# A gated cross-attention kernel on one Trainium2 core: two of its layer norms are computed inside the attention stages

## The reference

```python
def _layernorm(x, axis=-1, eps=1e-05):
    m = jnp.mean(x, axis=axis, keepdims=True)
    v = jnp.var(x, axis=axis, keepdims=True)
    return (x - m) / jnp.sqrt(v + eps)

x = x + jnp.tanh(g_xattn[0]) * _L0_xattn_ref(_layernorm(x), ctx_4096, Wq, Wk, Wv, Wo)
x = x + jnp.tanh(g_ffn[0]) * _L0_ffn_ref(_layernorm(x), W, b, Wq, Wk, A, Bm)
x = x + jnp.tanh(g_xattn[1]) * _L1_xattn_ref(_layernorm(x), ctx_4096, mask, Wq, Wk, Wv, Wo, q_norm_w, k_norm_w)
x = x + jnp.tanh(g_ffn[1]) * _L1_ffn_ref(_layernorm(x), ...)
```

```python
result = jnp.einsum('bsi,oi->bso', x, W) + b
q, k = x @ Wq.T, x @ Wk.T                    # (B, S, 8, 32) each
w = softmax(sum(q * k, -1) / sqrt(32), -1)
h = jnp.einsum('bsi,eri->bser', x, A)
return result + jnp.einsum('bse,bser,eor->bso', w, h, Bm)
```

## Time and profile before

| | us |
|---|---|
| median of 3 runs | 2628.84 (2624.82 to 2633.49) |
| profiled execution, whole | 2625.69 |
| its span, first to last instruction | 2623.9 |
| mean granted TensorE clock | 0.952 of 2.4 GHz |
| busy: PE, DVE, ACT, POOL | 2405.3, 1481.2, 1075.4, 995.0 |

### The profile page before, as it was taken

One profiled execution on the slowest core, in us unless ns is written; L12 is line 12 of the kernel. 1 busy time (PEld: TensorE's weight loads), 2 busy tenths in 40 slices (PEclk: granted clock), 3 DMA queues, 4 the chain that ended last, 5 costly groups with the idle time before them and its releaser, 6 DMA issues. The chain is left out here.

```text
span 2623.9 us, 34763 instructions
## 1 busy us (share of the span) xinstructions
PE 2405.3 (92%) x13032; PEld 2210.6 (84%) x13032; DVE 1481.2 (56%) x2352; ACT 1075.4 (41%) x2444; POOL 995.0 (38%) x812
## 2 busy tenths in 40 slices
PE   8999999979998899999879689999999999999724
PEld 6888888768998789998769578999999999999713
DVE  6222222132300566776677557777777777777797
ACT  3221222122311466667431245555555555554413
POOL 3000000000000446565253167667677677665110
PEclk9999999989999899999989899999999999999757
DMA  6222222143323223222213123333333333322001
GB/s 204 68 66 69 73 69 69 49 168 105 113 83 90 69 71 92 88 90 69 88 60 104 56 72 93 104 101 99 106 99 97 109 98 99 109 85 82 6 0 50
DMA packets 161240, 224.35 MB, mean 86 GB/s; under 512 B 31718, under 2 KB 124290, under 8 KB 160050
## 3 DMA queue, kind: packets, MB, share of 16 engines
q1 hardware_dynamic: 161074, 222.14, 27.2%
HBM read 183.81 MB, written 38.29 MB: 85 GB/s over the span
## 5 line engine op out<-in xcount | busy, mean ns | idle before, releaser
L967 POOL TENSOR_TENSOR attend_w_hi<-attend_w_raw,attend_one 128x1024 fp32r<-128x1024 f32 (+1 forms) x178 | 333.3, 1872 | 155.9 <-DMA attend_w_raw<-in_wo 81.5
L1146 DVE TENSOR_TENSOR attend_w_lo<-attend_w_raw,attend_w_hi 128x1024 fp32r<-128x1024 f32 (+1 forms) x184 | 252.4, 1372 | 206.3 <-ACT attend_w_hi L1034 123.1
L1284 PE MATMUL attend_ps_gemm<-normed_hi,attend_w_hi 128*128 128x400 f32 x704 | 246.5, 350 | 28.9 <-DVE attend_w_lo L1146 28.9
L1050 ACT ACTIVATE attend_p<-attend_p,attend_neg_max 100x361 f32<-100x361 f32 x256 | 150.9, 591 | 258.2 <-DVE attend_neg_max L1185 258.2
L1284 PE MATMUL attend_ps_gemm<-attend_o_hi,attend_w_hi 128*128 128x400 f32 x704 | 250.1, 355 | 4.4 <-issue 4.4
L1284 PE MATMUL attend_ps_gemm<-normed_lo,attend_w_hi 128*128 128x400 f32 x704 | 244.3, 347 | 0.0
L1284 PE MATMUL attend_ps_gemm<-normed_hi,attend_w_lo 128*128 128x400 f32 x704 | 243.5, 346 | 0.0
L1284 PE MATMUL attend_ps_gemm<-attend_o_hi,attend_w_lo 128*128 128x400 f32 x704 | 243.2, 346 | 0.0
L1284 PE MATMUL attend_ps_gemm<-attend_o_lo,attend_w_hi 128*128 128x400 f32 x704 | 243.2, 345 | 0.0
L301 DVE TENSOR_TENSOR context_k_square<-context_k_rows 128x512 f32<-128x512 f32 (+1 forms) x46 | 31.8, 691 | 346.7 <-ACT context_k_rows L226 346.6
L1059 ACT ACTIVATE attend_p<-attend_p,attend_exp_inv 100x361 f32<-100x361 f32 (+1 forms) x384 | 207.7, 620 | 0.0
(11 more groups left out here) (281 smaller groups left out, 6384.9 us busy)
## 6 DMA issues: line engine op xcount, KB each, us to landing
attend_w_raw<-in_wq SPq DMA_DIRECT2D x88, 512.0 KB, 4.0
attend_w_raw<-in_wo SPq DMA_DIRECT2D x64, 512.0 KB, 4.1
middle_w_raw<-in_wf SPq DMA_DIRECT2D x26, 512.0 KB, 3.5
attend_w_raw<-in_wo SPq DMA_DIRECT2D x32, 384.0 KB, 3.6
context_ctx_raw<-in_ctxT SPq DMA_DIRECT2D x8, 1456.0 KB, 7.2
attend_k_raw<-scratch_k SPq DMA_DIRECT2D x64, 180.5 KB, 3.6
context_ctx_raw<-in_ctxF SPq DMA_DIRECT2D x22, 512.0 KB
scratch_v<-context_v_out SPq DMA_DIRECT2D x44, 256.0 KB, 2.2
```

Of the source, the lines that this page charges most:

```text
L967: pool.tensor_tensor(hi, w_flat(w_raw, j % RAW, j), one[:hi.shape[0]].to_broadcast(hi.shape), ALU.mult).then_inc(w_hi_done, 1)
L1050: act.activation(p[:, slot, h], p[:, slot, h], ACT.Exp, bias=neg_max[:, slot, h:h + 1], accum_out=exp_sum[:, slot, h:h + 1]).then_inc(expe ...
L1146: dve.tensor_tensor(w_flat(w_lo, j % SPLIT, j), w_flat(w_raw, j % RAW, j), w_flat(w_hi, j % SPLIT, j).bitcast(F32), ALU.subtract).then_inc ...
L1284: mm = pe.matmul(out, left[a](c), right[b](c), start=(c == 0 and a == b == 0), stop=(c == chunks - 1 and a == 1))
```

## The change

The norms move by one half of the tokens. In layer 0's attention the units 18 to 31 compute the norm of the **first** half for the feed-forward, on POOL (sums, centring, scaling, remainders) and ACT (squares, root, rounding), with the reciprocal on DVE and two matmuls on PE. In `middle` remain two norms of four: that of the second half of its own input (made beside the first half's products) and that of the first half of layer 1's input (made beside the second half's products). In layer 1's attention the units 1 to 20 compute the norm of the **second** half of its own input, here with centring, scaling and remainders on DVE; the queries of that half start at unit 25 and wait for it. The mean and variance matmuls get places of their own in the ring of the two PSUM banks. Within `middle` the turn of the softmax weights moves from behind tile 5 to behind tile 6, `extra` starts behind tile 7, and DVE's list is reordered. POOL no longer waits for a norm ahead of its first weights.

```diff
+    if layer == 0:
+        NORM_HALF, C_SLOTS = 0, 4
+        ADD_AT, MEAN_AT, CENTRE_AT = (18, 19, 20, 20), 20, (21, 21, 22, 22)
+        SQUARE_AT, GATHER_AT, FOLD_AT = (22, 23, 24, 25), (24, 25, 26), 26
+        VAR_AT, INVERT_AT, SCALE_AT, HIGH_AT, LOW_AT = 26, 27, (27, 28, 28, 29), (28, 29, 29, 30), (30, 30, 31, 31)
+    else:
+        NORM_HALF, C_SLOTS = 1, 3
+        ADD_AT, MEAN_AT, CENTRE_AT = (1, 2, 3, 4), 5, (6, 7, 8, 9)
+        SQUARE_AT, GATHER_AT, FOLD_AT = (7, 8, 9, 10), (9, 10, 11), 12
+        VAR_AT, INVERT_AT, SCALE_AT, HIGH_AT, LOW_AT = 13, 14, (15, 16, 17, 18), (16, 17, 18, 19), (17, 18, 19, 20)
...
@@ attend, gpsimd @@
+            def add_tokens(k):
+                if layer == 0 and k < PAIRS - 1:
+                    pool.wait_ge(o_read, NU - 2 * HB + 4 + 2 * k)
...
+            def centre(k):
+                pool.wait_ge(mean_copied, 1)
+                pool.tensor_tensor(centred[:, k], norm_pair(tokens, k), norm_stat[:, 0].unsqueeze(1).to_broadcast([P, 2, HT]),
+                                   ALU.subtract).then_inc(centred_done, 1)
+
+            def scale(k):
+                pool.wait_ge(norm_inverted, 1)
+                pool.tensor_tensor(centred[:, k], centred[:, k], norm_stat[:, 1].unsqueeze(1).to_broadcast([P, 2, HT]), ALU.mult
+                                   ).then_inc(norm_scaled, 1)
...
                 for j in output_tiles(u + 1)[1:] + query_tiles(u + 1):
                     weights(j)
+                for k in range(PAIRS):
+                    if u == ADD_AT[k]:
+                        add_tokens(k)
+                    if k and u == GATHER_AT[k - 1]:
+                        add_squares(k)
+                if u == FOLD_AT:
+                    fold_squares()
+                if layer == 0:
+                    for k in range(PAIRS):
+                        if u == CENTRE_AT[k]:
+                            centre(k)
+                        if u == SCALE_AT[k]:
+                            scale(k)
+                        if u == LOW_AT[k]:
+                            remainder_normed(k)
                 squares(query_of(u))
@@ attend, scalar, at the end of a unit @@
+                for m in range(PAIRS):
+                    if u == SQUARE_AT[m]:
+                        square_centred(m)
+                    if u == HIGH_AT[m]:
+                        round_normed(m)
                 copy_q(query_of(u))
+                if u == MEAN_AT:
+                    copy_mean()
+                if u == VAR_AT:
+                    root_variance()
@@ attend, vector, at the end of a unit @@
+                if u == INVERT_AT:
+                    invert_root()
+                if layer == 1:
+                    for m in range(PAIRS):
+                        if u == CENTRE_AT[m]:
+                            centre(m)
+                        if u == LOW_AT[m]:
+                            remainder_normed(m)
+                        if u == SCALE_AT[m]:
+                            scale(m)
                 remainder_q(query_of(u))
@@ attend, tensor @@
+                if layer == 1 and n == G * QT:
+                    pe.wait_ge(ln_lo_done, PAIRS)
...
+            def norm_gemm(kind):
+                at = gemm_at[kind, 0, 0]
+                pe.wait_ge(norm_added, PAIRS if kind == "mean" else 2 * PAIRS)
+                bank_free(at)
+                pe.matmul(ps_gemm[:, at % 2, :HT], mean_w[:], norm_sum[:, 0], start=True, stop=True).then_inc(gemm_done, 1)
...
                 queries(query_of(u))
+                if u == MEAN_AT:
+                    norm_gemm("mean")
+                if u == VAR_AT:
+                    norm_gemm("var")
@@ middle, gpsimd @@
-            pool.wait_ge(ln_lo_done, PAIRS)
             for j in range(EARLY, EARLY + 3):
                 weights(j)
@@ middle, tensor @@
             pe.wait_ge(consts, CONSTS)
-            for c in range(NC):
-                mean_part(0, c)
-            mean(1)
-            variance_parts(0)
             for s in range(2):
                 for t in range(TILES):
                     product(s, t)
                     if s == 1 and t == 0:
                         extra(0, NC - 1)
-                    if s == 1 and t == 2:
-                        mean(2)
-                    if t == (3 if s == 0 else 7):
-                        variance(s + 1)
+                    if t == 1 + s:
+                        mean(s)
                     if t == QK:
                         score(s)
-                    if t == QK + 1:
+                    if t == QK + 2:
                         turn(s)
-                    if t > QK + 1:
+                    if t == QK + 3:
+                        extra(s, 0)
+                        extra(s, 1)
+                    if t > QK + 3:
                         extra(s, t - QK - 2)
-                    if s == 1 and t >= QK + 4:
-                        pe.wait_ge(o_read, NC + t - QK - 3)
-                        mean_part(3, t - QK - 4)
+                    if t == QK + 4:
+                        variance(s)
             extra(1, NC - 1)
-            for c in range(TILES - QK - 4, NC):
-                pe.wait_ge(o_read, NC + c + 1)
-                mean_part(3, c)
-            variance_parts(3)
```

317 lines of the change are left out of this document (188 added, 129 removed).

## The result

The changed kernel takes 2597.19 us (median of 4 runs, 2596.77 to 2599.51), the kernel before 2628.38 in the same comparison: 31.2 us less, ratio 0.9882 with a 95% interval of 0.9864 to 0.9899 (27 to 36 us). The forecast was 2590, 37 us less: the right size, 7 us too good, and just outside the interval.

The account below looks back on a forecast made before the run. PE bounds the attention stages, while serial chains starve it in three places of `middle`. Terms -45.9 + 6.5 + 2.4 = -37.0 us give 2588.7 from the profiled execution, 2591.8 from the median; forecast 2590, range 2577 to 2606 us.

Parts of the forecast that it names:

- Part 1: Start of `middle`: without norm 0, the first weight tile's remainder sets the products' start at 1307.8, 20.2 us earlier.
- the list of signs: What the changed profile should show, such as `middle`'s first product 7 to 8 us after the block's start.
- Part 2: Products of `middle`: 142.95 us become 137.7, with the `spread` wait gone and 6.4 us of new waits.
- Part 3: End of `middle`: next block begins at 1448.0 instead of 1493.95; 45.9 us saved in `middle`.
- Part 4: Layer 0's units 18 to 31: the added norm work is mostly covered and costs 6.5 us.
- my fourth rival: Layer 0's end: last two remainders behind POOL's last weights move the block's end up to 4 us; 2594 us; 0.62 with forecast.
- Part 5: Layer 1's units 1 to 20: the norm costs 2.4 us, 1.2 of it matmuls.
- The first: Rival: `middle` goes better and the cover in layer 0 holds; about 2581 us; chance 0.15.
- The second: Rival, both attention stages: each added POOL operation blocks a remainder 1.9 us, PE sees half; about 2611 us; chance 0.18.
- third: Rival: POOL becomes the bound of the attention units, so the kernel is slower; about 2642 us; chance 0.03.
- The -37.0: Whole kernel: sum of the stage terms, -45.9 + 6.5 + 2.4 us.

Follow-up runs that it names:

- no_norm3: Kernel before without norm 3, the norm behind the first feed-forward's last output tile for the next block's first half: 2606.73 us.
- Experiment 6: Changed kernel with POOL's last two norm remainders in layer 0's unit 31 moved ahead of the last output tiles' weights: 2596.48 us.
- experiment 12: Doses: changed kernel with one to four extra 128x800 additions on POOL or DVE in layer 1 units without norm work: 2603.86 us.
- the four moves: Changed kernel with unit 27's reciprocal and POOL's last layer 0 remainders earlier, `middle`'s squares sum behind tile 8's remainder, second-half mean one tile later: 2584.61 us.
- experiment 2: Changed kernel without the norm work in layer 0's units 18 to 31: 2588.03 us.
- experiment 3: Changed kernel without the norm work in layer 1's units 1 to 20: 2594.63 us.
- experiment 5: Changed kernel with DVE's reciprocal in layer 0's unit 27 moved ahead of its wait for o_hi: 2594.95 us.

## Why the prediction was nearly right

**Part 1, the start of `middle`: right.** By the sum the first product was to come 6.8 us behind the block's start, and it stands 6.3 behind it (the list of signs said 7 to 8, which didn't follow from the sum). That the first weights would be what is late next could be read from the rows of before.

**Part 2, the products: the term that was mis-sized.** I had 137.7 us, the profiled execution has 143.0 from first product to last add. The sum of the waits was right, 6.2 against 6.4 us, their places only in part: before tile 8 there are 2.43 and 1.21 (forecast 2.7 each), and 2.57 stand before the mean of the second half, which I had not as a wait at all. In the earlier trace rows the chain ran beside POOL; its shapes take 3.4 us alone and up to 8.3 beside three of POOL's roundings, so the one place came out shorter than I took it and the other appeared. What I left out wholly is the clock behind the waits. I allowed 1.6 us for it behind the wait that went, and nothing behind those that came. Two falls are 3.0 us of the 5.3 in this execution, the cold start another 0.9 (7.5 us for the first tile instead of 6.6). Another 0.9 is the last output tile's add: PE's last matmul starts at 1456.32, but DVE makes a remainder of the norm first and adds at 1457.60.

```profile
1456.32 0.35 PE L2006 MATMUL middle_ps_gemm<-middle_wh_hi,middle_bm_lo 128*128 128x400 f32 x1
1456.70 0.98 DVE L1852 TENSOR_TENSOR normed_lo<-middle_centred,normed_hi 128x800 fp32r<-128x800 f32 x1
```

In no_norm3, where nothing stands between, the add comes 0.4 us behind the start of that matmul. My sum had no term for this. Some 0.5 us I can't lay at a row. On average over six executions the stage is 150.9 us long where I had 147.0.

**Part 3, the end: right.** 2.9 us from the last add to the next block, forecast 2.5.

**Part 4, layer 0: the mechanism right, +8.2 instead of +6.5.** Unit 27 cost 3.15 (2.5 forecast) and is what the forecast named: the reciprocal ahead of `pt_lo`, and POOL waiting 13.60 us for it with the next weights and values behind it. Of these the values are what PE waits for, 1.06 us; the profile names no releaser, but POOL's remainder of them ends 0.1 us before.

```profile
1255.47 1.60 POOL L1031 TENSOR_TENSOR attend_v_lo<-attend_v_in,attend_v_hi 121x384 fp32r<-121x384 f32 x1
1257.16 0.40 PE L1534 MATMUL attend_ps_out<-attend_pt_hi,attend_v_hi 121*96 121x400 f32 x1 [1.06 <-issue]
```

The root's unit cost 0.92 (1.4). The timeline of ACT there:

```profile
1235.78 1.28 ACT L1209 ACT_TABLE_LOAD   x1
1237.07 0.59 ACT L1209 ACTIVATE attend_norm_stat<-attend_ps_gemm,attend_norm_eps 128x400 f32<-128x400 f32 x1
```

The root begins right behind the load, without a drain. So the price by the Trainium skill (ScalarE: Activation LUTs, What ACT_TABLE_LOAD costs), 2.66 us with the drain, was not paid where this trace can show it. Units 28 and 29 with their roundings cost 1.6 (1.3). What was missed is the tail, 1.7 us: my fourth rival had POOL's last two remainders too late for the block's end, but they did their harm earlier, by making DVE's last w_lo 2.64 us long. Experiment 6 takes them away and 1.2 us go.

**Part 5, layer 1: right.** The norm itself costs 1.8 us in the units (2.4 forecast), the two matmuls and units 17 and 18 with their three DVE operations each (0.10 and 0.25). That agrees with the doses, where two are free and the third is seen. Another 1.2 us at the stage's start are there without the norm's work too; I haven't settled from what, and executions of the new stage differ there by 1.8 us.

**The rivals.** The first (2581) was not this change but is about what the four moves make of it, 2584.6. The second and third fell with experiments 2, 3 and 12. What I gave for the second, the 1959 ns of the earlier trace rows, was misread: that row mixes two shapes. The 925 ns are of 128x768, which never took more than 0.96 us in that trace, and the 1959 are of 128x1024, which takes 1.19 alone. So the row shows a delay of 0.8 us, not one POOL operation of 1.9. Blocks of a whole operation and more are in the changed kernel (experiments 2 and 5), and PE sees little of them. The -37.0 came from one profiled execution of before. The difference of the two profiled executions is -28.3, that of the medians -31.2, since the profiled execution of before was 2.7 us below its median. In stretches whose code is the same the two differ by 1.0.
